# A fused two-layer gated block: the replicated queries of seven tiles sent through a DRAM scratch instead of straight from SBUF to SBUF

## The reference, cut to what matters

```python
x = x + tanh(g_x[0]) * diff_attention(ctx, layernorm(x))      # ATT0: 32 score maps of depth 8
x = x + tanh(g_f[0]) * routed_ffn(layernorm(x))               # FFN0: 3 of 8 zones per batch, 256 -> 1024 -> 256
x = x + tanh(g_x[1]) * attention(layernorm(x), ctx, ctx) @ Wo # ATT1: 16 heads of depth 16, with biases
x = x + tanh(g_f[1]) * gated_ffn(layernorm(x))                # FFN1: silu(gate) * up, 256 -> 768 -> 256
```

## Time and profile before

| | us |
|---|---|
| median of 3 runs | 679.21 (678.95 to 679.50) |
| the profiled execution | 679.59 |
| its span in the trace | 677.7 |
| PE busy | 614.7 (91%) |
| DVE busy | 386.6 (57%) |
| ACT busy | 361.1 (53%) |
| POOL busy | 147.5 (22%) |

### The profile page before, as it was taken

One profiled execution on the slowest core, in us unless ns is written; L12 is line 12 of the kernel. 1 busy time (PEld: TensorE's weight loads), 2 busy tenths in 40 slices (PEclk: granted clock), 3 DMA queues, 4 the chain that ended last, 5 costly groups with the idle time before them and its releaser, 6 DMA issues.

```text
span 677.7 us, 11609 instructions
## 1 busy us (share of the span) xinstructions
PE 614.7 (91%) x4332; PEld 504.3 (74%) x4332; DVE 386.6 (57%) x841; ACT 361.1 (53%) x614; POOL 147.5 (22%) x218
## 2 busy tenths in 40 slices
PE   2799888988799999999999999999878898999998
PEld 2565555555389899999989888989656776878887
DVE  6577677778573623425536534534586564656654
ACT  4317748566974745646557535535685433543421
POOL 9622365154650000000000000000374310210000
PEclk9779999989899999999999999999999998999999
DMA  7311021122022030030303250020041100000000
GB/s 232 98 56 42 25 52 24 48 50 96 3 86 71 1 125 1 8 117 1 125 1 95 55 164 1 1 95 2 10 131 48 50 0 2 33 1 8 25 32 32
DMA packets 22552, 34.76 MB, mean 51 GB/s; under 512 B 4705, under 2 KB 13281, under 8 KB 22497
## 3 DMA queue, kind: packets, MB, share of 16 engines
q1 hardware_dynamic: 20224, 30.51, 14.6%
q0 software_dynamic: 1984, 3.44, 2.1%
q10 hardware_dynamic: 288, 0.07, 0.1%
HBM read 18.93 MB, written 2.10 MB: 31 GB/s over the span
## 4 chain that ended last, share of the span: by engine, by line
PE 75%; DVE 10%; ACT 6%; POOL 4%; issue 3%; DMA 1%; SPq 0%; ACTq 0%; DVEq 0%; POOLq 0%
PE PV L1239 22%; PE SC L1267 20%; PE SC L1239 9%; PE AUX L1239 4%; PE PV L1258 4%; PE AUX L1349 3%; PE SC L1379 3%; PE PV L1267 2%; DVE NM L1114 2%; PE AUX L1267 2%; DVE O L1122 2%; ACT XN L838 2%; PE AUX L1306 1%; ACT PB L889 1%; PE PV L1349 1%
## 5 line engine op out<-in xcount | busy, mean ns | idle before, releaser
L975 DVE TENSOR_TENSOR HL<-HF,HH 128x512 fp32r<-128x512 f32 x96 | 67.2, 700 | 154.6 <-ACT HH L931 154.5
L889 ACT ACTIVATE PB<-SC 77x1024 f32<-77x1024 f32 x96 | 95.2, 1014 | 59.6 <-PE SC L1379 59.5
L1267 PE MATMUL SC<-WBH,HL 128*128 128x256 f32 x384 | 108.7, 283 | 0.0
L1267 PE MATMUL SC<-WBL,HH 128*128 128x256 f32 x384 | 108.6, 283 | 0.0
L1267 PE MATMUL SC<-WBH,HH 128*128 128x256 f32 x384 | 108.6, 283 | 0.0
L931 ACT ACTIVATE HH<-PV 128x512 fp32r<-128x512 f32 x96 | 57.3, 597 | 71.8 <-PE SC L1267 71.8
L926 ACT ACTIVATE HF<-PV 128x512 f32<-128x512 f32 x96 | 57.5, 599 | 54.7 <-PE PV L1239 52.6
L703 POOL TENSOR_TENSOR RSTD<-RSTD,NHALF 128x4 f32<-128x4 f32 x16 | 17.8, 1115 | 291.5 <-DVE RSTD L1049 291.4
L1239 PE MATMUL PV<-XH,WAH 128*128 128x512 f32 x192 | 77.5, 404 | 1.0 <-DVE O L1122 1.0
L1267 PEld LDWEIGHTS SC<-WBL,HH 128*128 128x128 f32 x384 | 72.7, 189 | 3.9
L1267 PEld LDWEIGHTS SC<-WBH,HH 128*128 128x128 f32 x384 | 72.5, 189 | 4.0 <-DVE HL L975 0.4
(11 more groups left out here) (250 smaller groups left out, 1230.9 us busy)
## 6 DMA issues: line engine op xcount, KB each, us to landing
QG<-QH SPq DMA_DIRECT2D x96, 64.0 KB, 2.0
WSA<-in_wa SPq DMA_DIRECT2D x6, 1024.0 KB, 5.0
WSB<-in_wb SPq DMA_DIRECT2D x12, 512.0 KB, 6.7
QG<-QL SPq DMA_DIRECT2D x48, 64.0 KB, 2.0
X<-in_x SPq DMA_DIRECT2D x4, 512.0 KB, 6.8
QG<-QH POOLq DMA_DIRECT2D x32, 64.0 KB, 2.3
out_x<-X SPq DMA_DIRECT2D x8, 256.0 KB, 2.3
QG<-QL POOLq DMA_DIRECT2D x16, 64.0 KB, 2.2
```

What stands on the lines that cost most here:

```text
L889: act.activation(probs(n)[0:S, :, :], scores(n)[0:S, :, :], ACT.Exp, scale=SCALE[a]).then_inc(exp_done, 1)
L975: return dve.tensor_tensor(dst, raw, hi.bitcast(F32), ALU.subtract)
L1267: ins = pe.matmul(ps[:, D * (t % 2):D * (t % 2 + 1)], lhs[:, block], rhs, start=first and t == 2 * i and n == 0, stop=last and t == 2 * i ...
```

## The change: what it does

`BOTH` becomes `(0,)`: only tile 0 is moved as before. For tiles 1 to 7 a DRAM tensor `QD` of 2 MB stands between. At the step `q_move` of half 0, SP waits for both halves of the query (and, from n = 2 on, for the loads of tile n - 1), and stores each half with one DMA of 512 KB, high and low part together; `QH` and `QL` are now two views of one tensor `QHL`, in which they lie side by side in a partition. Then, for each half, SP waits as before for `sc_ready`, waits for the store to have landed (`q_kept`), and issues three loads of 256 KB, one for each of the three copies. POOL issues nothing for these tiles. ACT, before it writes the next tile's `QH`, waits for the store alone.

```diff
-BOTH = (0, 1, 6, 7)
+BOTH = (0,)
...
+        QD = nc.dram_tensor("queries", [KC, P, 2, NT], F32).ap()
...
-        QH = place("QH", [P, KC, NT], F32R)
-        QL = place("QL", [P, KC, NT], F32R)
+        QHL = place("QHL", [P, KC, 2, NT], F32R)
+        QH, QL = (QHL[:, :, i, :] for i in range(2))
...
-            eng.wait_ge(q_moved[n % 2][c], 16 * sum(6 if m in BOTH else 12 for m in range(n % 2, n + 1, 2)))
+            eng.wait_ge(q_moved[n % 2][c], 16 * sum(6 if m in BOTH else 3 for m in range(n % 2, n + 1, 2)))
             if n in BOTH:
                 eng.wait_ge(pool_moved[n][c], 16 * 6)
...
-                    if n >= 2:
-                        sp.wait_ge(sc_ready, unit((n - 2) // J, (n - 2) % J, 0) + units[(n - 2) // J] * (c + 1) // KC)
+                    if n not in BOTH:
+                        if c == 0:
+                            for k in range(KC):
+                                used(sp, ("query", a, j, k))
+                                if n - 1 not in BOTH:
+                                    sp.wait_ge(q_moved[(n - 1) % 2][k], 16 * sum(6 if m in BOTH else 3 for m in range((n - 1) % 2, n, 2)))
+                                sp.dma_start(QD[k], QHL[:, k, :, :].bitcast(F32)).then_inc(q_kept[k], 16)
+                        if n >= 2:
+                            sp.wait_ge(sc_ready, unit((n - 2) // J, (n - 2) % J, 0) + units[(n - 2) // J] * (c + 1) // KC)
+                        sp.wait_ge(q_kept[c], 16 * n)
+                        for q, part in enumerate((0, 1, 0)):
+                            sp.dma_start(QG[n % 2][32 * q:32 * q + 32, 4 * c:4 * c + 4, :].bitcast(F32),
+                                         QD[c][:, part, :].rearrange("(r p) n -> p r n", p=32)).then_inc(q_moved[n % 2][c], 16)
+                        continue
                     used(sp, ("query", a, j, c))
-                    for r in range(2 if n in BOTH else 4):
+                    for r in range(2):
...
-                    if n:
+                    if n - 1 in BOTH:
                         query_moved(act, n - 1, c)
+                    elif n:
+                        act.wait_ge(q_kept[c], 16 * (n - 1))
```

More of the change, by code:

```diff
@@ L496, in flamingo @@
         m_moved = [[sem(f"m_moved{i}{g}") for g in range(G)] for i in range(2)]
-        stored = sem("stored")
+        stored, q_kept = sem("stored"), [sem(f"q_kept{c}") for c in range(KC)]
         aux_ready = sem("aux_ready")
```

## The result

| | before | after |
|---|---|---|
| median of 20 runs each, us | 678.37 (677.31 to 679.56) | 680.71 (678.60 to 682.89) |
| ratio after / before | | 1.0035, 95% interval 1.0027 to 1.0043 |
| the profiled execution, us | 679.59 | 682.48 |
| its span, us | 677.7 | 680.6 |
| mean granted TensorE clock | 0.977 | 0.972 |

The change costs 2.3 us, more than the 0.2% that can be told from no change. The page after, first the shares of the span in the chain that ended last, then the DMA issues (tile, queue, count, KB each, median us to landing). A tile is stored in two DMAs of 512 KB, so `QD` holds 1 MB and not the 2 MB said above.

The account below looks back on a forecast made before the run. The kernel was taken as PE-bound, with transfers hardly ever ending a wait. Profiled span 677.7 + 1.1 (tile 7 wait) - 0.5 (POOL) = 678.3, giving 679.8 us for the median, +0.6; range 677.2 to 682.4.

Parts of the forecast that it names:

- the first rival: Slower outcome: tile 7's first `max` waits up to 2.8 us; 682.0, up to 683.7 with low clock; chance 0.30.
- Where it can bite: Only tile 7's first `max` waits for a `QG` load; it had 0.9 us of slack, tiles 1 to 6 enough.
- Store 3.0: SP's 512 KB store of a query half to DRAM takes 3.0 us, bounds 2.3 and 4.0.
- Three loads 4.7: Three loads of 768 KB together, each into 32 partitions, take 4.7 us, bounds 4.2 and 5.4.
- Wait +1.1: PE waits 1.1 us at tile 7's first `max`, bounds 0 and 2.8, all of it on the path.
- The way: From the query's low part through store and loads to the first half in `QG`: 7.8 us, ends 6.5 and 9.5.
- POOL -0.5: At tile 6, POOL without DMAs does `X += BOG` earlier, `WGL` shortens: -0.5 us, bounds 0 and -1.3.
- Clock 0: A half-clock stretch drawn or removed by PE's shifted idle time: value 0, bounds -1.7 and +1.7 us.
- Issue time removed 0: Fewer DMA issues on SP are worth nothing, as nothing on PE's path waits for SP's issue.
- Rows up to 480 us stay within 0.2 of their places: Sign of a right forecast: timeline rows before 480 us shift by no more than 0.2 us.

Follow-up runs that it names:

- experiment 1: Changed kernel with tile 7 moved directly by SP and POOL, tiles 1 to 6 still through DRAM: 677.25 us against 678.60 for the kernel before, ratio 0.9982.
- experiment 2: Kernel before with tile 7 alone sent through DRAM: 681.62 us, ratio 1.0045.
- experiment 4: Changed kernel with the store of tile 7's second half issued behind its first half's loads: 679.70 us, ratio 1.0021 to the kernel before.
- experiment 5: Kernel before with tile 6 moved directly by SP alone, POOL issuing nothing there: 678.08 us against 678.74, ratio 0.9993.
- experiment 6: Kernel before with POOL's `X += BOG` placed ahead of its moves of tile 6: 677.70 us against 678.74, ratio 0.9990.
- experiment 8: Kernel before with eight useless matmuls on PE in its 2.0 us wait for ACT before tile 7's first `max`: 677.31 us, ratio 0.9989.
- experiment 9: Changed kernel with eight useless matmuls in PE's wait for ACT and eight in its wait for tile 7's load: 679.04 us, ratio 1.0006 to the kernel before.
- experiment 11: Kernel before with tiles 1 to 6 moved directly by SP alone, tile 7 by SP and POOL, eight useless matmuls in PE's ACT wait: 679.44 us, ratio 1.0013.
- experiment 10: Changed kernel with tile 7 moved directly and eight useless matmuls in PE's wait for ACT: 675.63 us, ratio 0.9964 to the kernel before.
- experiment 7: Changed kernel with tile 7's first `max` ordered one attend later: 679.42 us against 678.68 for the kernel before, ratio 1.0013.

## Why the prediction was right in its range and wrong in its forecast

The time lies inside the range (677.2 to 682.4), but the forecast was +0.6 and no change that can be measured; what came is the first rival, the `max` of tile 7 that waits long. Of the forecast's 679.8 us, 0.8 came from the three runs at hand, whose median lay that much above the median of twenty (679.21 against 678.37), so the miss is 1.7 us of difference and not only the 0.9 of the times. Two terms of the sum failed: the three loads, which were mis-sized, and the clock, which was put at nothing. Step by step:

- **Where it can bite: right.** Tile 7's first `max` waits, no `max` of tiles 1 to 6 does. Experiments 1 and 2 show it from both sides.
- **Store 3.0: 2.7 measured**, within its bounds. The 2.3 of the 256 KB stores was the near row. That HBM stores signal late, which the Trainium skill ("Perfetto Trace Analysis", section "DMA Instruction — HWDGE (DVE, Sync)") warns of, no run here shows.
- **Three loads 4.7: this term was mis-sized.** It was 6.1, beyond its upper end of 5.4. The bound took the loads as alone on the DMA engines. They were not: the other half's store was issued just ahead of them, which experiment 4 prices at 0.3 to 0.7, and `NMT`'s moves ran among them. Even without that store they took 5.5, the upper end of the term. The windows of 1 us in the changed kernel show the loads' rate at full engines, and their tail:

```profile
524.00:525.00 1.00, 0.00 (x0) 0.00 (x0) 0.00 (x0) 1.00 (x2) 0.00 (x0) 1.00 0.99 234
525.00:526.00 1.00, 0.71 (x2) 0.30 (x2) 0.50 (x1) 0.59 (x2) 0.00 (x0) 1.00 1.01 223
526.00:527.00 1.00, 0.00 (x0) 0.00 (x0) 0.19 (x1) 0.89 (x1) 0.00 (x0) 1.00 0.29 64
```

  The rate that the prediction took from direct moves, 229 GB/s, was near enough; the time beside the bytes and the company were not. From 526 on only 64 GB/s moved, and the last load landed at 527.89. By the rule on the partitions 0 to 31 in the Trainium skill ("SBUF — State Buffer", section "Door 1: The DMA port swizzle") the estimate was 6.2 for the loads. The traces agree with its direction (223 to 234 GB/s here, 398 in the earlier trace rows). That its total comes near the 6.1 is luck: the 189 GB/s behind it is the page's reading for a whole transfer of 1 MiB, to which the prediction added 2.0 us of landing, while the bytes here moved at 223 to 234 and the rest of the 6.1 was landing and sharing.
- **Wait +1.1: 2.1 measured** (1.66 and 1.37 in experiments 2 and 4). The way was 8.9 in place of 7.8, and that is the whole of the difference.
- **POOL -0.5: right.** -0.5 in the profiled pair; -0.7 and -1.0 by medians in experiments 5 and 6, and the 1.6 to 1.7 of experiments 8 and 9 leave 0.4 to 0.5 for it. `WGL` took 2.77 to 2.79 in the three profiles where it ran beside POOL's `X += BOG`, and 0.96 in the ten where it did not. The rule of the Trainium skill ("SBUF — State Buffer", section "Who interferes with whom") that a DVE instruction with two SBUF inputs contends with a GpSimd instruction that reads SBUF agrees with all of them.
- **Clock 0: a term put at nothing, and it was not nothing.** The prediction asked whether the grown idle time would be followed by another low stretch and took 0, since no row could tell. One came: 527.5 to 534.4 at 0.50, which cost 1.8 us in the profiled execution. In the mean of the runs it is some 0.6, most likely because the kernel before has a shorter stretch there too in part of its runs: three of the five profiled kernels without the load wait and without a filler have it. That share is not measured. With the way at 8.9 and no clock the sum is 2.1 - 0.5 = 1.6, just at the edge of what can be measured; with that 0.6, which was itself taken from the measured times, it is 2.2.
- **Issue time removed 0: right for this kernel, but no general rule.** Experiment 11 shows the condition: it is worth 1.9 us where SP alone would have the direct moves ahead of `NMT`. The kernel before avoided it by `BOTH`.
- **"Rows up to 480 us stay within 0.2 of their places": wrong** by 0.6 to 0.7, but such a shift is what two executions differ by.

The slower rival had the right mechanism, and its condition, a way over about 8.6 us, is what decided. Its price of 682.0 was for the way at 9.5.

What stays open: experiment 1 gains 1.35 us, of which POOL's freed time at tile 6 explains 0.5 to 1.0. The rest has no wait that answers to it, and may be noise: either gain is known to some 0.5 us. Nor is it settled why experiment 10 has only 24.3 us of low clock in all five of its runs, when the filler alone and the direct tile 7 alone had 30: in its profile there is no low stretch between 54 and 490, where each of the other twelve has one or two. The two gains added up to 3.1, where 2.8 was the sum. And the price of a low stretch is only roughly known: from the changed kernel to experiment 9, 6.7 us less of it went with 1.7 less span; from experiment 1 to 10, 6.1 with 1.2.

## What to carry to other kernels

Look for the one place with the least slack before a change that makes every transfer longer: six of the seven tiles had room for the longer way, and the seventh had 0.9 us to spare and set the result. Bound a chain of transfers with what else is issued around it on the same engines, also by the change itself. And where PE stands still behind another wait already, price a longer gap above its length; the cheap remedies are to leave that one tile on the short way, and to fill the gap with work.

## What the runs showed of the hardware that had not been expected

- A store of 512 KB from 128 partitions to DRAM was done 2.7 us after its issue (median of 14), hardly more than 256 KB (2.3). Three loads of 256 KB into 32 partitions each took 5.5 us with little beside them (experiment 4) and 5.7 to 6.1 with another store in flight (five profiles).
- The same 2.00 us of PE idle behind ACT were followed by the full clock (the kernel before, experiment 7) or by 3.4 us at half of it (experiments 1, 5 and 6). With 2.1 us of idle time more there were 6.8 us at half, and the mean low clock of a run rose from 31 to 36 us; with the idle time filled by useless matmuls it fell to 29, and in experiment 10 to 24.
- DMA issues of POOL beside a DVE operation with two SBUF inputs cost DVE nothing (0.96), POOL's own `tensor_tensor` beside it made it 2.79.
